# State space layer of a 12-layer kernel: C selected between two sums, B three units ahead, and a reordered first pass

## The reference

```python
dbc = jnp.einsum('bld,ed->ble', u, Wx)            # dt (64), B (16), C (16)
delta = jax.nn.softplus(jnp.einsum('blr,dr->bld', dt, Wdt) + bdt)
dA = jnp.exp(delta[..., None] * A)
dBu = delta[..., None] * Bm[:, :, None, :] * u[..., None]
def step(h, inp):
    dA_t, dBu_t, C_t = inp
    h = dA_t * h + dBu_t
    y = jnp.einsum('bdn,bn->bd', h, C_t)
    return (h, y)
return ys.transpose(1, 0, 2) + u * D
```

## Time and profile before

| | us |
|---|---|
| median of 3 runs | 4833.25 (4831.69 to 4837.05) |
| profiled execution, its own time | 4826.13 |
| its span in the trace | 4824.3 |
| first scan of the state space layer | 93.3 |
| stretch of its units | 93 to 1260 |
| mean granted TensorE clock over the span | 0.918 |

### The profile page before, as it was taken

How to read it: one execution, slowest core, us unless ns; L and a number is a source line. 1 busy time by engine, 2 the same in 40 slices (tenths; PEclk the granted TensorE clock), 3 DMA queues, 4 the chain that set the end, 5 groups by cost and what they waited for, 6 DMA issues and landing times.

```text
span 4824.3 us, 59405 instructions
## 1 busy us (share of the span) xinstructions
PE 4088.0 (85%) x21276; PEld 2776.0 (58%) x21276; DVE 3205.9 (66%) x7409; ACT 2179.8 (45%) x5294; POOL 1353.9 (28%) x876
## 2 busy tenths in 40 slices
PE   5677877867799996999899998788798779778989
PEld 2222323323466775998788886455565558436767
DVE  3878888888765665666688896566576654534751
ACT  3554655646444441222233336467676532423331
POOL 2776767678300000000122223364220000100011
PEclk8888988989999997999999999789899989878999
DMA  1000000000000000000000000000000000000000
GB/s 48 0 0 0 0 0 0 1 0 0 37 1 1 1 1 38 27 18 10 12 1 1 1 1 37 12 1 1 11 2 2 1 36 1 36 0 18 1 1 18
DMA packets 9176, 45.79 MB, mean 9 GB/s; under 512 B 715, under 2 KB 5939, under 8 KB 6451
## 3 DMA queue, kind: packets, MB, share of 16 engines
q1 hardware_dynamic: 8883, 42.00, 2.4%
HBM read 39.90 MB, written 2.10 MB: 9 GB/s over the span
## 4 chain that ended last, share of the span: by engine, by line
PE 33%; DVE 12%; ACT 4%; issue 2%; POOL 1%; DMA 0%; DVEq 0%; ACTq 0%; POOLq 0%
PE PS L208 27%; PE PS L215 4%; DVE qg L1885 1%; ACT p L2363 1%; DVE stat L285 1%; PE PS L2867 1%; DVE p L3146 1%; DVE qg L1880 1%; DVE XNr L322 1%; ACT p L3159 1%; DVE sm L1396 1%; DVE wc L3071 0%; DVE p L2594 0%; DVE p L3311 0%; DVE sm L2592 0%
## 5 line engine op out<-in xcount | busy, mean ns | idle before, releaser
L1018 DVE TENSOR_TENSOR_SCAN db<-PS,db 128x512 f32<-128x512 f32 x512 | 593.0, 1205 | 81.5 <-ACT PS L986 46.4
L208 PE MATMUL PS<-db,cst 128*128 128x512 f32 x1024 | 520.3, 647 | 0.0
L215 PE MATMUL PS<-cst,p 128*128 128x128 f32 (+1 forms) x2880 | 398.2, 285 | 54.2 <-DVE pt L2831 23.6
L1701 POOL TENSOR_TENSOR rb<-rb,tb 128x512 f32<-128x512 f32 x32 | 41.2, 1287 | 1341.4 <-DVE tb L1696 1341.4
L208 PE MATMUL PS<-part,selb 96*128 96x512 bf16 x512 | 179.8, 410 | 270.2 <-DVE db L1025 191.6
L215 PEld LDWEIGHTS PS<-cst,p 128*128 128x128 f32 (+1 forms) x2880 | 339.3, 150 | 106.3 <-issue 38.0
L208 PE MATMUL PS<-xnT,W 128*128 128x256 f32 (+1 forms) x1184 | 381.6, 470 | 21.2 <-ACT pt L2389 8.8
L966 POOL TENSOR_TENSOR db<-W,b 128x1024 f32<-128x1024 f32 x128 | 311.6, 2445 | 153.1 <-PE PS L208 67.9
L966 POOL TENSOR_TENSOR db<-du,b 128x1024 f32<-128x1024 f32 x128 | 302.3, 2374 | 135.4 <-PE PS L208 80.7
L208 PEld LDWEIGHTS PS<-db,cst 128*128 128x128 f32 x1024 | 215.0, 210 | 208.7 <-issue 193.3
L208 PEld LDWEIGHTS PS<-xnT,W 128*128 128x128 f32 x1184 | 232.0, 200 | 160.4 <-issue 114.6
(11 more groups left out here) (423 smaller groups left out, 9056.5 us busy)
## 6 DMA issues: line engine op xcount, KB each, us to landing
W<-in_we SPq DMA_DIRECT2D x9, 1024.0 KB, 4.8
W<-in_w SPq DMA_DIRECT2D x1, 4224.0 KB, 13.0
W<-in_w SPq DMA_DIRECT2D x1, 4122.5 KB, 14.8
W<-in_w SPq DMA_DIRECT2D x1, 4100.0 KB, 12.0
W<-in_w SPq DMA_DIRECT2D x1, 2770.0 KB, 15.5
W<-in_w SPq DMA_DIRECT2D x1, 2313.0 KB, 9.3
X<-in_x SPq DMA_DIRECT2D x4, 512.0 KB, 5.8
W<-in_w SPq DMA_DIRECT2D x1, 2048.0 KB, 8.0
```

Source lines behind the costliest of these rows:

```text
L208: ins = T.matmul(out, l, r, start=first and i == 0, stop=last and i == len(pairs) - 1)
L215: ins = T.transpose(bank[0:m, c:c + r], s, ident[0:r, 0:r])
L1018: V.tensor_tensor_scan(db[:, f, r], self.ring.PS[:, self.BANKS[x % 3], r], db[:, f, r], 0.0, ALU.mult, ALU.add).then_inc(self.sc.sem, 1)
```

## The change

- `steps`: step i now issues the B part of unit i, exp(delta*A) of unit i-2, and scan, C and sum of unit i-3. The db buffers are six in place of five. The pieces stay at their step numbers, so they come one unit earlier as seen from the scans.
- `pe_tail`: where GpSimd has the product of unit t, the selection of C for unit t+1 is issued in step t between the two sums, instead of in the next step. It waits for ScalarE's copy of C of unit t.
- The first pass: the first tokens are loaded ahead, then Win in a load of its own, the context, the other weights, and the remaining tokens last. The tokens' normalisation is issued before the context's on every engine. The projection and convolution begin with blocks 2 and 3, whose convolution (chunk 0 alone) goes from TensorE to VectorE, four operations per block. SiLU and softplus of chunk 0, direction 0, run in halves; its subtraction goes from GpSimd to VectorE.

```diff
+            if c == 0 and self.first:
+                e.eng.dma_start(E.region(0)[:, 0:2048], A["w0"][:, 0:2048]).then_inc(self.win.sem, 16)
+            if c == 0 and self.context:
+                e.eng.dma_start(self.raw[0:S2], A["ctx"].rearrange("b s d -> s b d")).then_inc(self.ctx_in.sem, 16)
+            if c == 0:
+                E.load_weights(e, LAYERS[0], 2048 if self.first else 0)
...
+        for s in range(32):
+            self.nxt.dve(e, s, self.nxt.early)
         if self.context:
             self.dve_context(e)
...
-        self.db = [E.tile(f"db{i}", 1024) for i in range(5)]
+        self.db = [E.tile(f"db{i}", 1024) for i in range(6)]
...
+    FIRST = (2, 33, 3, 34, 8, 10, 0, 31, 1, 32, 4, 5, 35, 6, 7, 36, 12, 13, 14, 15, 16, 39, 17, 40, 18, 41, 19, 42, 20, 21,
+             EXP, BCA, LN, PART, PART + 1, MAX, SUB, ADD, DU)
...
+    def halves(self, k):
+
+        return [(slice(0, 2), 1), (slice(2, 4), 2)] if k == 0 else [(slice(0, 4), k + 2)]
...
-        for i in range(self.NU + 4):
+        for i in range(self.NU + 5):
             norm(e, i, self.inn.late)
             nxt(e, i, self.nxt.early)
             if i < self.NU:
                 one(e, i)
-            if 0 <= i - 1 < self.NU:
-                two(e, i - 1)
-            if 0 <= i - 2 <= self.NU:
-                three(e, i - 2)
+            if 0 <= i - 2 < self.NU:
+                two(e, i - 2)
+            if 0 <= i - 3 <= self.NU:
+                three(e, i - 3)
...
+            if c == 0 and f >= 2:
+                return
...
+                e.wait_ge(*self.uv(2))
+                C.activation(self.u[:, 1024:2048], self.u[:, 1024:2048], ACT.Silu).then_inc(self.silus.sem, 1)
+                e.wait_ge(*self.ua(2))
+                C.activation(self.u[:, 0:1024], self.u[:, 0:1024], ACT.Silu).then_inc(self.silus.sem, 1)
+                return
...
+            for r, x in self.halves(k):
+                C.activation(v4(self.t1)[:, r, :], v4(delta)[:, r, :], ACT.Abs).then_inc(e.own, e.up())
             e.wait_ge(e.own, e.ups)
-            C.activation(self.t1, self.t1, ACT.Exp, scale=-1.0).then_inc(self.ee.sem, 1)
+            for r, x in self.halves(k):
+                t = v4(self.t1)[:, r, :]
+                C.activation(t, t, ACT.Exp, scale=-1.0).then_inc(self.ee.sem, 1)
...
-            e.wait_ge(*self.ln(k + 1))
-            V.scalar_tensor_tensor(self.t2, delta, 0.0, self.t2, ALU.max, ALU.add).then_inc(e.own, e.up())
-            e.wait_ge(e.own, e.ups)
-            V.tensor_scalar(delta, self.t1, 1.0, -1.0, ALU.add, ALU.add).then_inc(self.qm.sem, 1)
-        elif j == self.ADD:
-            e.wait_ge(*self.sp_(k + 1))
-            V.tensor_tensor(delta, self.t2, self.t1, ALU.add).then_inc(self.dl.sem, 1)
+            for r, x in self.halves(k):
+                t1, t2, dl = [split(a, 4)[:, r, :] for a in (self.t1, self.t2, delta)]
+                e.wait_ge(*self.ln(x))
+                V.scalar_tensor_tensor(t2, dl, 0.0, t2, ALU.max, ALU.add).then_inc(e.own, e.up())
+                e.wait_ge(e.own, e.ups)
+                V.tensor_scalar(dl, t1, 1.0, -1.0, ALU.add, ALU.add).then_inc(self.qm.sem, 1)
+                if k == 0:
+                    e.wait_ge(*self.qm(x))
+                    V.tensor_tensor(t1, t1, dl, ALU.subtract).then_inc(e.own, e.up())
+                    e.wait_ge(e.own, e.ups)
+                    V.tensor_tensor(dl, t2, t1, ALU.add).then_inc(self.dls.sem, 1)
+        elif j == self.ADD and k:
+            e.wait_ge(*self.sp_(k))
+            V.tensor_tensor(delta, self.t2, self.t1, ALU.add).then_inc(self.dls.sem, 1)
+        elif self.CONV <= j < self.SILU and k == 0 and j % 2 == 0 and j >= self.CONV + 4:
...
+            for i in range(4):
+                w, x = self.conv[:, f, i:i + 1], self.up[:, f, :, i:i + S]
+                if i == 0:
+                    ins = V.tensor_scalar(u, x, w, self.W["bconv"][:, f:f + 1], ALU.mult, ALU.add)
+                else:
+                    e.wait_ge(e.own, e.ups)
+                    ins = V.scalar_tensor_tensor(u, x, w, u, ALU.mult, ALU.add)
+                if i < 3:
+                    ins.then_inc(e.own, e.up())
+            ins.then_inc(self.uv.sem, 1)
...
-            e.wait_ge(*self.dl(k + 1))
             e.wait_ge(*self.silu(c + 1))
             e.wait_ge(*self.gb(self.ends(k - 2)))
-            G.tensor_tensor(self.du[d], self.delta[d], self.u, ALU.mult).then_inc(self.du_.sem, 1)
+            for r, x in self.halves(k):
+                e.wait_ge(*self.dls(x))
+                G.tensor_tensor(split(self.du[d], 4)[:, r, :], split(self.delta[d], 4)[:, r, :],
+                                split(self.u, 4)[:, r, :], ALU.mult).then_inc(self.dus.sem, 1)
...
-        e.wait_ge(*self.du_(k + 1))
-        e.wait_ge(*self.sum_of(i - 5))
-        e.eng.tensor_tensor(split(self.db[i % 5], 2), split(self.du[d], 4)[:, 2 * p:2 * p + 2, :],
+        e.wait_ge(*self.du_(k + 1, p if k == 0 else 1))
+        e.wait_ge(*self.sum_of(i - 6))
+        e.eng.tensor_tensor(split(self.db[i % 6], 2), split(self.du[d], 4)[:, 2 * p:2 * p + 2, :],
...
+    def pe_c(self, e, i):
+        c, p, d, k, s = self.of(i)
+        if i:
+            e.wait_ge(*(self.ca(self.pools(i)) if self.on_pool(i - 1) else self.made(i - 1)))
+        mm(e.eng, self.ring.PS[:, self.CBANK, :], [(self.sel_c[0:96, 16 + s, :], self.part[d][0:96, :])]).then_inc(
+            self.pc.sem, 1)
+
     def pe_tail(self, e, i):
 
-        T = e.eng
-        if i < self.NU:
-            c, p, d, k, s = self.of(i)
-            if i:
-                e.wait_ge(*(self.ca(self.pools(i)) if self.on_pool(i - 1) else self.made(i - 1)))
-            bank = self.ring.PS[:, self.CBANK, :]
-            mm(T, bank, [(self.sel_c[0:96, 16 + s, :], self.part[d][0:96, :])]).then_inc(self.pc.sem, 1)
-        for j in self.sums(i):
+
+        if i < self.NU and not (i and self.on_pool(i - 1)):
+            self.pe_c(e, i)
+        for x, j in enumerate(self.sums(i)):
             e.wait_ge(*self.made(j))
             self.pe_sum(e, j)
+            if x == 0 and i < self.NU and self.on_pool(i):
+                self.pe_c(e, i + 1)
```

More of the change, by code:

```diff
@@ L435, in over @@
     def over(self):
-        return self.E.ctx_ready
+        return [] if self.first else self.E.ctx_ready
     def sp(self, e):
@@ L455, in dve @@
         V.memset(E.one, 1.0).then_inc(self.z.sem, 1)
+        for s in range(32):
+            self.nxt.dve(e, s, self.nxt.early)
         if self.context:
             self.dve_context(e)
-        for s in range(32):
-            self.nxt.dve(e, s, self.nxt.early)
     def dve_context(self, e):
@@ L489, in act @@
         e.wait_ge(*self.z(1))
+        for s in range(32):
+            self.nxt.act(e, s, self.nxt.early)
         if self.context:
             self.act_context(e)
-        for s in range(32):
-            self.nxt.act(e, s, self.nxt.early)
     def act_context(self, e):
@@ L507, in pe @@
     def pe(self, e):
+        for s in range(32):
+            self.nxt.pe(e, s, self.nxt.early)
         if self.context:
             self.pe_context(e)
-        for s in range(32):
-            self.nxt.pe(e, s, self.nxt.early)
     def pe_context(self, e):
@@ L649, in setup @@
         self.nth = [order.index(i) + 1 for i in range(n)]
-        self.todo = [[] for _ in range(n + 4)]
+        self.todo = [[] for _ in range(n + 5)]
         one = {self.DT: 0, self.DT + 1: 1, self.DTA: 2, self.BC: 7, self.BC + 1: 8, self.EXP: 8, self.BCA: 9,
@@ L676, with dl, du_, silu @@
     UP, UA, DLA = 31, 35, 39
[L677 to L678 removed]
+    SOFT = (EXP, LN, MAX, SUB, ADD, DU)
+    FIRST = (2, 33, 3, 34, 8, 10, 0, 31, 1, 32, 4, 5, 35, 6, 7, 36, 12, 13, 14, 15, 16, 39, 17, 40, 18, 41, 19, 42, 20, 21,
+             EXP, BCA, LN, PART, PART + 1, MAX, SUB, ADD, DU)
+    def dl(self, k, half=1):
+        return self.dls(k + half if k > 0 else 0)
+    def du_(self, k, half=1):
+        return self.dus(k + half if k > 0 else 0)
+    def silu(self, k):
+        return self.silus(k + 1 if k > 0 else 0)
+    def halves(self, k):
+        return [(slice(0, 2), 1), (slice(2, 4), 2)] if k == 0 else [(slice(0, 4), k + 2)]
     def on_pool(self, i):
@@ L870, in act_piece @@
                 e.wait_ge(*self.sum_of(64 * (c - 1) + 32))
-            e.wait_ge(*self.cv(4 * c + f + 1))
+            else:
+                e.wait_ge(*self.w_ready)
+                for token in self.E.ctx_ready:
+                    e.wait_ge(*token)
+            e.wait_ge(*self.cv(4 * c + f - 1 if c else f + 1))
             C.activation(v4(self.u)[:, f, :], ring.of(("conv", c, f)), ACT.Identity,
@@ L975, in act_da @@
         c, p, d, k, s = self.of(i)
-        e.wait_ge(*self.dl(k + 1))
+        e.wait_ge(*self.dl(k + 1, p if k == 0 else 1))
         e.wait_ge(*self.Ar(1))
```

67 lines of the change are left out of this document (39 added, 28 removed).

## The result

The changed kernel takes **4893.58 us** (4884.22 to 4896.35, four runs) against 4832.84 for the kernel before on the same chip: a ratio of 1.0121, 95% interval 1.0103 to 1.0138, some 61 us slower. I had said 4793, with 4834 as the upper end. Its profiled execution took 4891.55, with a span of 4889.7.

What follows compares the result with a forecast made beforehand. No engine was full, VectorE nearest (968.4 of 1167 us). Terms +12.6 - 5 + 6 - 27 - 13 - 14 = -40 on the profiled 4826.1 gave 4786, plus 7 for the median: 4793 us, range 4760 to 4834.

Steps and rivals of the forecast that it cites:

- It only shifts which pieces meet a pair of sums.: Units: the lead of three only changes which groups have a piece behind two sums, 23 before, 19 now.
- 19 x 11.50: Middle units of the chunks: 19 groups of three with a piece behind two sums, 11.50 us each, before 10.87.
- C between the sums, +0.3 quiet and +0.6 with a piece.: Units: earlier C selection delays the second sum, next B and exp(delta*A); us added per three units.
- 12.6 + 6: Units: +12.6 us over 40 steady groups, +6 for 20 quiet groups among the softplus stages.
- above 60: Sign to look for: VectorE's waits for exp(delta*A) rise from 46 to above 60 us, on scans of R.
- B three units ahead does not loosen this.: Units: the lead leaves exp(delta*A) behind a B copy issued after the same sums, so no relief.
- Stages at steps 55 to 60, -27.: Three softplus stages: fewer GpSimd operations inside VectorE's work, no 3.69 wait for the B product; -9 us each.
- rival (a'): Eight softplus stages: one more GpSimd product of 2.35 us inside VectorE's work, +19, giving 4813; chance 0.10.
- Stages at steps 8 to 13, -13: Four stages: a unit more slack less exp(delta*A)'s delay, -1.7 each; transposes' wait shrinks 2.2 each over three; -13 us.
- y, -5: Wait for the last sum before y: one projection piece fewer ahead of it in three chunks, -5 us.
- First pass, -14.: Start of the layer: earlier Win and shorter convolution bring the first scan from 93.31 to 79, -14 us.
- (c): Rival: ScalarE's copy of C, on which the second sum hangs, sets the pace; slower, 4867; chance 0.14.

Runs made afterwards that it cites:

- e3_neither: Changed kernel with the lead of three and C between the sums both undone, only the first pass new: 4811.49 us, ratio 0.9958.
- e2_noc: Changed kernel with the C selection back at the head of its own step, lead of three kept: 4855.35 us, ratio 1.0049.
- e8_pieces_early: As e3_neither, but every piece issued one step earlier (step 0's pieces stay): 4856.89 us, ratio 1.0053.
- e4_shift1: Changed kernel whole, but every piece and norm step in the state space layer issued one step later: 4860.37 us, ratio 1.0059.
- e1_nolead: Changed kernel with the lead of three undone (five db buffers again), C between the sums kept: 4862.50 us, ratio 1.0068.
- e9_mixed: As e7_lead_aligned, but the last softplus pieces at steps 55 to 60 stay at their own step numbers, one unit earlier: 4793.66 us, ratio 0.9929.
- e7_lead_aligned: As e2_noc, but every piece issued one step later: 4804.47 us, ratio 0.9953.
- e10_shift2: As e7_lead_aligned, but every piece two steps later than in the changed kernel in place of one: 4775.31 us, ratio 0.9886.

## Why the prediction was wrong

The 61 us are -20 (first pass, e3_neither), +44 (place -1, e2_noc against e3_neither) and +38 (C between the sums, the changed kernel against e2_noc); with the last two taken in the other order they are +51 and +31. By its steps:

**"It only shifts which pieces meet a pair of sums."** This is the step that failed. I counted groups with a piece behind a *pair* of sums, found 23 before and 19 now, and took that for a small gain. I priced the piece by whether it is in the way of a B behind two sums, as if the step with one sum and the step with none were alike. They aren't. A convolution has two halves in neighbouring steps. Before, one of them stood in the empty step, where no row shows it costing anything; now both stand behind sums and TensorE is idle in the empty one. The earlier trace rows shows the one behind the pair (274.74), and that was all I read. The other half stood one step further in the same timeline of the kernel before, behind no sum:

```profile
276.89 1.88 PE L208 MATMUL PS<-tt,W 128*128 128x512 f32 x4
```

The term was "19 x 11.50"; measured with lead and C it is 13.17 and 14.59, and 14.02 without C. All of place -1 is +44, where my count of 19 in place of 23 alone was a gain of 5.5 (four groups at 9.49 in place of 10.87). 26 of it stand in the convolution stretches that this chain explains, 17 in the gate stretches (by e8_pieces_early, 43 in all). And I had the clock as a constant (0.88), where it hangs on this very order.

**C between the sums, +0.3 quiet and +0.6 with a piece.** Both sizes were right: 9.73 against 9.78, and with the pieces in place 0 11.45 against 11.50 (e4_shift1). What failed is that I took them for the whole price. I read how late ScalarE's copy of C is in one quiet stretch (+3.05) and took that for all groups. It stands behind whatever ScalarE has: in the gate stretch units 16 to 31 lose 8 us, and behind the SiLU it comes 4.11 us late and takes the clock along. So the term was 12.6 + 6 and came to 51 (e1_nolead against e3_neither) or 38 (in place -1, where part of it may be hidden behind waits that are there anyhow; that isn't shown). The direction, that the wait moves from the product to the scan, was right: 70.4 to 18.1, and 46.4 to 190.6, where I had said "above 60".

**"B three units ahead does not loosen this."** Right as to the lead alone: by the medians it is worth 2 and 7 us at places -1 and 0, no more than the intervals of those runs, and 15 at place +1; by the start of the last unit's scan 2, 6 and 2. It never costs by itself.

**Stages at steps 55 to 60, -27.** The operations moved as said. Unit 54 to unit 62 took 53.5 before and takes 46.9 now, -6.6 against -9 said, and the wait of 3.69 for the B product is gone. But it is one of three: the other two took 48.1 and 47.5 before and take 47.8 and 47.0, so all three gave 7.4. And the three whole stretches of sixteen units around them take 271.5 us in place of 258.4 (e2_noc: 256.2), so C between the sums took more there than the moved operations gave. By e9_mixed the three are worth some 7 to 11 us. The term was three times the one stage that I had read. A row of that stage in the changed kernel, and what remains of the collisions there:

```profile
367.46 2.72 POOL L1075 TENSOR_TENSOR db<-db,c 128x1024 f32<-128x1024 f32 x1 [5.19 <-ACT c L1068]
...
368.01 2.46 DVE L967 CAST part<-r 32x512 bf16<-32x512 f32 x1
...
374.88 4.42 DVE L982 TENSOR_TENSOR W<-tt 128x2048 f32<-128x2048 f32 x1 [0.72 <-POOL tt L1012]
```

A product of GpSimd beside the cast (2.46 in place of 0.42), and the addition 4.42 in place of 2.29 beside two more. That is the mechanism of rival (a'), the rule of the Trainium skill (SBUF — State Buffer, section Who interferes with whom) that these rows bear out. Its size can be read from the view by lines, group L962 (busy us, mean ns), of e3_neither:

```profile
L962 DVE CAST part<-r 32x512 bf16<-32x512 f32 x14 | 14.1, 1007 | 0.5
```

and of the changed kernel:

```profile
L962 DVE CAST part<-r 32x512 bf16<-32x512 f32 x14 | 24.5, 1752 | 0.5
```

By this and the like VectorE's busy time in the stretch of the units is 966.7 in e3_neither, 984.5 in e2_noc, 986.1 in e8_pieces_early and 996.7 in the changed kernel: 18 to 20 us more at place -1, near the 19 that I had for it. That the numbers meet is luck. Mine was eight products of 2.35 us in the way, and what shows is longer operations of VectorE; e2_noc's softplus stretches take 256.2 us all the same, and e3_neither's 258.5. So busy time was added; how much of the kernel's time it cost isn't shown.

**Stages at steps 8 to 13, -13; y, -5.** The y wait fell by 5.0, as said. Units 0 to 15 take 95.2 against 90.3, and over the four chunks these stretches take 372.9 against 364.9: a loss of 8 where I had a gain of 13. Without C between the sums the lead gives 5 or 6 of it (359.7 in e2_noc, 358.8 in e7_lead_aligned). C between the sums costs 7.6 there at place 0 (366.4 in e4_shift1) and 13.2 at place -1.

**First pass, -14.** Measured -11.8 with the lead and -15.1 without it: right within its ends. Its parts:

```profile
30.65 7.11 PE L210 MATMUL PS<-tt,W 128*128 128x512 f32 x16 [1.27 <-ACT tt L894]
...
67.70 3.18 POOL L1018 TENSOR_TENSOR W<-W 128x1024 f32<-128x1024 f32 x1 [66.86 <-DVE W L979]
...
68.72 2.72 DVE L974 TENSOR_SCALAR W<-tt 128x1024 f32<-128x1024 f32 x1
...
78.76 0.60 ACT L1031 ACTIVATE b<-PS 128x512 f32<-128x512 f32 x1 [10.31 <-POOL db L1038]
```

Win at 21.35 (said 21.4), the convolution 7.11 (said 6.95), the first half's L972 at 63.08 (said 61.6 for its place). The second half's operation at 68.72 takes 2.72 in place of 0.69 beside GpSimd's first half (67.70); I had that as possible. And the third B copy waits 10.31 and stands ahead of the table load, as priced: +3.0 by e3_neither and e7 (78.16 and 81.12), +2.8 said.

**The rivals.** (c) was the one on the right side: ScalarE's copy of C, on which the second sum hangs. It was worked out to 4867 and given 0.14, and would have been right for half of the loss. No rival had the pieces in it, and so all were too low and the range ended 60 us short. The range took its bounds for the units from 0 to +25; both bounds were made of the same rows of quiet and convolution groups. It also left out my own bad ends: +19 on 4833 is 4852, still 42 us short.

## What to carry to other kernels

Where an order is written out by step numbers, moving one stream by a step moves every fixed piece against the pattern of the others. Write the pattern down (here two, none, one sums) and put each piece against it before and after, also those pieces that no line of the diff names; then try all places of the period, since here it gave 80 us between the worst and the best (without C between the sums), and a version 1.1% faster than the kernel before (e10_shift2). And a short instruction that is slipped in between two others brings its wait along: look for the latest time that its partner is ready anywhere, behind table loads and long activations, and not for the time it is ready in a quiet stretch.

## What the runs showed of the hardware

Standstills of TensorE as short as 2.27 us (with 0.13 us busy in 2.40) were followed by a clock of 0.6 over the next 3.5 us, and one of 4.11 us by 0.50 over 4.4 us. I had not expected it of gaps so short. It doesn't follow each time: of two equal standstills of 2.48 us in the changed kernel one was followed by 1.00 and the other by 0.57. Over all units the mean hardly moves, 0.87 against 0.88. TensorE's busy time says more, as its instructions are nearly the same in number: 871.9 us in e3_neither, 886.5 in e2_noc, 883.8 in e8_pieces_early and 912.3 in the changed kernel. So as an estimate from these rows the clock accounts for up to 12 to 15 of the 44 us of place -1; in the one group that I read it is half of the excess, and the share itself stays open. Not tried: a second PSUM bank for C, which would let C be selected without the copy, and the parts of the first pass one by one.
